# Sixteen-batch attention and expert layer on one core: the last two shared parts summed on chip, ten pieces behind the last expert

## What is computed

```python
x = x + xattn(layernorm(x), ctx, mask, Wq, Wk, Wv, Wo)
h = layernorm(x)                                   # 4096 rows of 512
topk_idx, topk_w = gate(h)                         # 4 of 32 experts for each row
out = moe(h, topk_idx, topk_w, w1, w2, w3)         # each expert: 128 slots, 512 -> 256 -> 512
shared = silu(h @ shared_gate) * (h @ shared_up) @ shared_down
x = x + out + shared
```

## Time and profile before

| | us |
|---|---|
| median of 3 runs | 1621.64 |
| lowest and highest | 1621.61, 1622.02 |
| the profiled execution, its own time | 1623.28 |
| its span, first to last instruction | 1621.3 |

### The profile page before, as it was taken

The page is one execution under the profiler, slowest core; times in us unless marked ns, Lnnn a source line. Parts: engine busy times, 40 slices in busy tenths (PEclk is TensorE's granted clock), DMA queues, the critical chain, the costliest instruction groups (busy, mean ns, idle before and its releaser), DMA issues. The chain is left out here.

```text
span 1621.3 us, 33869 instructions
## 1 busy us (share of the span) xinstructions
PE 1599.5 (99%) x11431; PEld 1074.6 (66%) x11431; DVE 1218.7 (75%) x3520; ACT 846.9 (52%) x2090; POOL 797.8 (49%) x1096
## 2 busy tenths in 40 slices
PE   8999999999999999999999999999999999999997
PEld 5666666666666676666666666667677766666663
DVE  7988787878778787878787787878866257767773
ACT  6765445545545445454544544545444256666672
POOL 3443646465564646464555646464346534334323
PEclk9999999999999999999999999999999999999998
DMA  8765455354555445544545454454466578988935
GB/s 258 187 155 114 106 98 112 72 118 82 117 99 112 97 107 105 98 113 90 127 80 124 93 119 101 95 111 87 105 195 205 128 223 215 271 242 219 268 66 65
DMA packets 399659, 218.21 MB, mean 135 GB/s; under 512 B 348400, under 2 KB 356592, under 8 KB 399488
## 3 DMA queue, kind: packets, MB, share of 16 engines
q1 hardware_dynamic: 383024, 189.71, 47.3%
q0 software_dynamic: 15904, 25.29, 9.3%
q10 hardware_dynamic: 560, 1.05, 0.2%
HBM read 91.87 MB, written 40.80 MB: 82 GB/s over the span
## 5 line engine op out<-in xcount | busy, mean ns | idle before, releaser
L968 ACT ACTIVATE arena<-arena,neg_max 128x256 f32<-128x256 f32 x512 | 253.7, 496 | 377.6 <-DVE neg_max L1277 377.6
L711 POOL TENSOR_SCALAR arena<-arena,prob_scale 128x256 f16<-128x256 f32 x384 | 185.2, 498 | 470.6 <-DVE prob_scale L1286 468.6
L1651 PE MATMUL ps_query<-xn_both,arena 128*128 128x256 f16 x1024 | 279.1, 273 | 0.8 <-DMA xn_both<-xn_half 0.8
L1653 PE MATMUL ps_query<-xn_both,arena 128*128 128x256 f16 x1024 | 279.1, 273 | 0.0
L1652 PE MATMUL ps_query<-xn_both,arena 128*128 128x256 f16 x1024 | 279.1, 273 | 0.0
L1294 DVE SCALAR_TENSOR_TENSOR arena<-arena,prob_scale 128x256 f16<-128x256 f32 x384 | 239.4, 672 | 9.2 <-POOL arena L711 8.9
L1277 DVE CUSTOM_DVE_ANT_0 arena<-ps_score,mask_add 128x256 f32<-128x256 f32 x512 | 186.2, 419 | 79.6 <-PE ps_score L1653 79.6
L1651 PE MATMUL ps_out<-arena,o_t 128*128 128x512 f16 x512 | 194.1, 379 | 0.7 <-DVE o_t L1299 0.7
L1652 PE MATMUL ps_out<-arena,o_t 128*128 128x512 f16 x512 | 194.1, 379 | 0.0
L1653 PE MATMUL ps_out<-arena,o_t 128*128 128x512 f16 x512 | 194.0, 379 | 0.0
L761 POOL DMA_INDIRECT slot_table<-entry,slot_at x128 | 130.0, 1015 | 47.9 <-issue 33.8
(11 more groups left out here) (337 smaller groups left out, 3961.1 us busy)
## 6 DMA issues: line engine op xcount, KB each, us to landing
arena<-w SPq DMA_DIRECT2D x96, 512.0 KB, 6.3
out_rows_dram<-weight_in POOLq DMA_DIRECT2D x32, 256.0 KB, 5.5
x_in<-x SPq DMA_DIRECT2D x15, 512.0 KB, 3.9
out_rows_dram<-x SPq DMA_DIRECT2D x30, 256.0 KB, 2.4
xn_rows<-xn_half SPq DMA_DIRECT2D x15, 512.0 KB, 3.1
x2t_kept<-xn_both SPq DMA_DIRECT2D x12, 512.0 KB, 2.9
ctx_in<-ctx_t SPq DMA_DIRECT2D x16, 256.0 KB, 3.1
weight_in<-wq SPq DMA_DIRECT2D x8, 512.0 KB, 5.4
```

The lines of the kernel that those rows point to most:

```text
L711: pool.tensor_scalar(p_rows[:, 0, c, :], probs[:, c, :], prob_scale[:, c:c + 1], 1.0, ALU.mult, ALU.mult).then_inc(norm_hi, 1)
L968: act.activation(probs[:, c, :], probs[:, c, :], ACT.Exp, bias=neg_max[:, c:c + 1], scale=-1.0, accum_out=prob_sum[:, c:c + 1]).then_inc(e ...
L1651: pe.matmul(dst, a.hi, b.hi, start=start and n == 0, stop=False)
L1653: m = pe.matmul(dst, a.lo, b.hi, start=False, stop=stop and n == len(pairs) - 1)
```

## The change

The four down pieces of the last two batches (FINAL, pieces 92 to 95) go another way. SP waits for all row adds, reads the 4 x 128 rows back from `out` into `final_rows` (a part of `weight_in` that is free by then), VectorE adds the piece from its PSUM bank to them (`final_summed`), and SP stores the sums to `out` with plain DMAs and waits for the stores. ScalarE's copies and POOL's accumulating DMAs of these pieces are gone. The four pieces have a bank each: the two score banks and the two fill banks. LAST becomes 10: pieces 86 to 95 stand behind the last expert, and experts 25 and 26 have none beside them.

```diff
-LAST = 6
+LAST = 10
 BEHIND = range(len(PIECES) - LAST, len(PIECES))
+FINAL = range(len(PIECES) - 2 * TB, len(PIECES))
...
+        final_rows = [weight_in[1][:, n * D:(n + 1) * D] for n in range(2 * TB)]
...
         def piece_bank(k):
+            if k in FINAL:
+                return (ps_score + ps_fill)[FINAL.index(k)]
             if k in BEHIND:
                 return ps_fill[k % 2]
...
+        def final_at(k):
+            _, n, t = PIECES[k]
+            return LATE[n] * T + t * P
...
-        additions += [("s", n) for n in range(behind, len(LATE))]
...
             sp.wait_ge(added_first, 16 * TB)
             sp.wait_ge(added, adds_total)
+            sp.wait_ge(pe_up, ups(PIECES[FINAL[0]][1] - 1, FSB))
+            for n, k in enumerate(FINAL):
+                sp.dma_start(final_rows[n], out[final_at(k):final_at(k) + P, :]).then_inc(in_final[n], 16)
+            for n, k in enumerate(FINAL):
+                sp.wait_ge(final_summed, n + 1)
+                sp.dma_start(out[final_at(k):final_at(k) + P, :], final_rows[n]).then_inc(out_final, 16)
+            sp.wait_ge(out_final, 16 * len(FINAL))
...
-            for n in range(behind, len(LATE)):
-                add_shared(n)
...
-            for k in BEHIND[1:]:
+            for k in BEHIND[1:-len(FINAL)]:
                 piece(k)
                 piece_high(k)
...
-            for k in BEHIND:
+            for k in BEHIND[:-len(FINAL)]:
                 piece(k)
                 piece_rest(k)
+            for n, k in enumerate(FINAL):
+                _, m, t = PIECES[k]
+                dve.wait_ge(pe_down, downs(m, t) + 1)
+                dve.wait_ge(in_final[n], 16)
+                dve.scalar_tensor_tensor(final_rows[n], piece_bank(k)[:, :], 1.0 / (HS_S * W_S), final_rows[n], ALU.mult,
+                                         ALU.add).then_inc(final_summed, 1)
...
-                if k > BEHIND[1]:
+                if k in FINAL[2:]:
+                    pe.wait_ge(*piece_emptied(FINAL[0] - 1))
+                elif k in FINAL:
+                    pe.wait_ge(ehid, E)
+                elif k > BEHIND[1]:
                     pe.wait_ge(*piece_emptied(k - 2))
```

More of the change, by code:

```diff
@@ L303, in build @@
         out_x2t = signal("out_x2t")
+        in_final = [signal(f"in_final{n}") for n in range(2 * TB)]
+        final_summed, out_final = signal("final_summed"), signal("out_final")
         in_x2t = [signal(f"in_x2t{n}") for n in range(KEPT)]
@@ L445, in build @@
         ahead = min(staged_in)
-        behind = max(staged_in) + 1
+        assert max(staged_in) == PIECES[FINAL[0]][1] - 1
         additions = [("s", n) for n in range(1, ahead)]
@@ L450, in build @@
             additions += [("x", e - 1), ("x", e - 2)]
-        additions += [("s", n) for n in range(behind, len(LATE))]
-        assert len(additions) == E + len(LATE) - 1
+        assert len(additions) == E + len(LATE) - 3
         adds_done, adds_before, total = {}, {}, 0
@@ L455, in at_once @@
             kind, n = what
-            return kind, n // 2 if kind == "x" else min(n, behind)
+            return kind, n // 2 if kind == "x" else n
         for (kind, _), together in groupby(additions, key=at_once):
```

## The result

| | before | changed |
|---|---|---|
| median, us | 1621.83 (6 runs) | 1616.35 (6 runs) |
| lowest and highest | 1621.1, 1622.84 | 1615.93, 1617.08 |
| span of the profiled execution | 1621.3 | 1614.1 |

The ratio is 0.9965 (95% interval 0.9954 to 0.9977), 5.5 us or 0.35% less, and the interval leaves out 1. The same two kernels on another chip, later, gave 1623.68 and 1617.67, a ratio of 0.9963 (0.995 to 0.9977), 6.0 us less. The forecast was 1615.5, or 6.1 us less.

A forecast was written before the change was run, and what follows sets the result against it. Bound by TensorE, busy 1599.5 of 1621.3 us, plus the tail behind its last matmul. TensorE's end 1611.5 plus tail 3.7 gave span 1615.2, 6.1 us less; median 1621.64 - 6.1 = 1615.5, range 1613.9 to 1618.9.

The forecast's parts named there:

- Moved pieces, +1.0 us: Experts 25 and 26 lose the cover of four pieces; TensorE ends 1.0 us later, bounds 0 and 2.2.
- No gaps in the pieces behind the last expert: Pieces behind expert 31 alternate between two banks without waiting: cost nothing, at most 0.8 us.
- POOL's closing leaves the path: At the program's end, POOL's 9.7 us drain starts after an earlier row add and ends at 1602, under TensorE's pieces.
- The sum 0.69, handovers, store: Tail behind the last matmul: sum 0.69, handovers 0.04 and 0.1, store 2.4, closing 0.3 and 0.2; 3.7 us against 10.8.
- The read-back is covered: Before the final sums: row adds through at 1596 to 1598, loads take 5.5 us, last there by 1603.5; cost nothing.
- The base: Gain taken from the profiled span of 1621.3 us, then carried over to the median of 1621.64.
- The end did not keep its price: Rival at the program's end: SP's closing takes the 4.7 us in its turn, median 1619.9; chance 0.11.
- The adds were not late: Rival: serial row adds delay the read-back and set the end if landing from 1606 on; chance 0.04.
- The dearer bare experts: Rival in experts 25 to 28: 3 us lost in place of 1.0, median 1617.5; counted within the forecast's 0.80.

The follow-up runs named there:

- less_split: Changed kernel with VectorE's low-half split of the second weight third cut to 128 of 1024 columns for experts 27 to 31: median 1617.49 us.
- pool_last_store: Changed kernel with the last of the four final stores issued by POOL instead of SP, plain: median 1622.41 us, ratio 0.9994.
- The second trace: The kernel before, unchanged, run and profiled once more: median 1621.9 us, ratio 1.000, span 1619.9.
- the late and the early DMA: Changed kernel plus one 32 KB read by POOL, issued after the last final piece (median 1621.92 us) or after the first (1617.11).

## Why the prediction was right, point by point

The forecast was 1615.5 us, in a range of 1613.9 to 1618.9; measured were 1616.35.

- *Moved pieces, +1.0 us.* Right in size: +1.03 in the change, +1.02 in the move alone. It was taken between 0.81 and 1.18. The bound was named only half: VectorE as the one that sets a bare expert's time. The runs show ScalarE as a second bound of the same height. The price was taken from rows, so the wrong name did it no harm; a remedy built on it would have failed, as `less_split` shows.
- *No gaps in the pieces behind the last expert.* Right: behind expert 29's gate product the four pieces add 10.48 us, 4 x 2.62, and the last three sums wait for TensorE 1.90 us each.
- *POOL's closing leaves the path.* Right, and the largest single term. The prediction let the drain run 9.7 us from POOL's last DMA; it is the landing plus 4.6. Both end long before the new tail, so the sum did not change.
- *The sum 0.69, handovers, store.* 0.69 to the hundredth. The store was mis-sized: 2.4 predicted, 2.0 measured; the handover to SP took 0.03 for 0.1. The tail is 3.2 for 3.7, a little under its lower bound of 3.4, which rested on the shortest of thirty stores made beside other traffic (2.3). The estimate of 2.6 us beside it comes from the page "DMA: Bandwidth & Descriptors" of the Trainium skill, section "Anatomy of one DMA — SWDGE (gpsimd) path", which is about DMAs issued by GpSimd and not by SP. The run to hold it against is `pool_last_store`: 2.4 us.
- *The read-back is covered.* Right: adds through at 1596.8 by SP's first load (predicted 1596 to 1598), the first sum ends its wait on TensorE at 1603.14. The load of 1 MB took 5.0 us in the kernel without the move, for an estimate of 5.5.
- *The base.* The sum was made against an execution with a tail of 10.8 us; carrying its difference of 1.6 us over to the median assumed that all of that lay outside the terms. The second trace, whose span is 1.4 us shorter, has 0.4 us of that in the tail and 1.0 ahead of expert 25. So the new tail was forecast 0.5 too long and the old one taken 0.4 too long for the median, and that these two nearly cancel is luck. From expert 25 on the traces give 6.1 to 6.7 us less, the medians 5.5 and 6.0. The rest, 0.1 to 1.2 us, must lie ahead of expert 25, where two traces of the same kernel differ by 1.0 us; whether it is scatter stays open.
- *The rivals.* The end did not keep its price: SP's drain was 7 ns directly behind its last landing. It keeps it where POOL's last DMA is still young, as the late and the early DMA tell apart. The rule of the Trainium skill, page "VectorE: DVE Perf Modes", section "The DRAIN you can't avoid", is about the DRAINs of the preamble and postamble, some 57 to a kernel and about 12 ns each on all engines. The closing DRAINs here are one to an engine, at the kernel's own line 102 or 103, so the prediction probably held the rule against another instruction than it is about: only SP's (7 ns) fits it, while POOL's took 6.9 to 11.4 us in all traces here, ScalarE's 0.44 to 0.63 and VectorE's 0.46 to 0.73. Of the last two the prediction said that they close at once. The adds were not late. The dearer bare experts did not come.

What the prediction did not ask is which part of the change brings the gain. The read-back brings all of it: alone it is 6.0 us under the kernel before, with the move 5.5 and 6.0, and in the traces 0.4 us faster without the move. The move costs 1.03 us of TensorE and buys 0.60 us of cover.

## What to carry to other kernels

Read the end of a program to its last row, past the last landing: an engine's closing can hold it, and here a DMA in POOL's queue held the end for 4.5 to 4.7 us behind its landing, be it an add or a plain store of 256 KB or a read of 32 KB. Let the last transfer be one of SP's, and let POOL's last DMA be issued early: here its drain ended 6.9 to 9.7 us behind the issue. And price cover on both sides: here moving work to hide a transfer took the cover from two experts, which was dearer (1.03 us) than the wait that it hid (0.60).

## What the runs showed of the hardware that was not expected

- POOL's closing DRAIN ends 4.5 to 4.7 us behind the landing of its last DMA near the end: 5.0 and 9.7, 4.6 and 9.25, 4.1 and 8.76 (adds of 256 KB), 2.5 and 7.1, 2.6 and 7.1 (a read of 32 KB), 2.4 and 6.9 (a plain store of 256 KB). In the changed kernel, whose last DMA by POOL is a row add, the drain is over 4.3 us behind SP's first load, which waits for that add (1601.2 and 1596.86). SP's takes 7 ns behind a store that has just landed.
- A plain store of 256 KB lands in 2.4 us from POOL and 2.0 us from SP with idle queues; 128 KB from SP in 1.7. An accumulating one of 256 KB takes 4.0 to 4.1 us with an empty queue before it, and 4.6 to 5.4 behind two that were issued together.
- Work taken from VectorE alone was worth 0.28 us, from ScalarE alone 0.66 us, and from both at once 2.02 us.
